# Expert layers: one ScalarE copy brings all three weight blocks of a slot, and VectorE takes over the copy of the turned rows

## The reference

```python
def _L0_ffn_ref(x, gate, experts_w1, experts_w2, experts_w3):      # layers 2 and 4: 8 experts, best 2 of a token
    routing_weights, selected = jax.lax.top_k(jnp.einsum('bsh,he->bse', x, gate), 2)
    ...
    g = jnp.einsum('bsh,ehi->ebsi', x, experts_w1)                 # 128 -> 512
    u = jnp.einsum('bsh,ehi->ebsi', x, experts_w3)                 # 128 -> 512
    eo = jnp.einsum('ebsi,eih->ebsh', silu(g) * u, experts_w2)     # 512 -> 128
    out = jnp.einsum('ebsh,bse->bsh', eo, tok_w)
```

## Time and profile before

| | us |
|---|---|
| three runs | 2781.56, 2788.8, 2790.41 (median 2788.8) |
| the profiled execution | 2790.66, its span 2788.9, mean granted clock 0.884 |
| slots of the four expert layers (first to last transposition or matmul of a slot) | 133 to 362, 545 to 775, 1710 to 1823, 2656 to 2770 |

### The profile page before, as it was taken

One profiled execution on the slowest core, in us unless ns is written; L12 is line 12 of the kernel. 1 busy time (PEld: TensorE's weight loads), 2 busy tenths in 40 slices (PEclk: granted clock), 3 DMA queues, 4 the chain that ended last, 5 costly groups with the idle time before them and its releaser, 6 DMA issues. The chain is left out here.

```text
span 2788.9 us, 78885 instructions
## 1 busy us (share of the span) xinstructions
PE 2227.6 (80%) x30447; PEld 1572.1 (56%) x30447; DVE 1813.1 (65%) x5841; ACT 1398.5 (50%) x3584; POOL 897.8 (32%) x904
## 2 busy tenths in 40 slices
PE   6499947699935888888888877948899888888686
PEld 3288835388812333333333335836777777777486
DVE  6633357633355776767867634359999999999622
ACT  5455543455521554454544445536556555555453
POOL 2156643166541101000000003534444444444254
PEclk7699979699965998988988887969999999999898
DMA  4111120111143211110110001121111111111112
GB/s 125 36 41 42 43 70 1 39 42 42 42 139 93 63 31 35 33 43 18 43 33 22 15 1 52 42 82 53 52 51 53 48 49 50 45 49 49 40 39 89
DMA packets 76684, 134.93 MB, mean 48 GB/s; under 512 B 17892, under 2 KB 32926, under 8 KB 73886
## 3 DMA queue, kind: packets, MB, share of 16 engines
q1 hardware_dynamic: 62742, 102.07, 11.6%
q0 software_dynamic: 13568, 27.81, 3.4%
q10 hardware_dynamic: 8, 0.00, 0.0%
HBM read 65.19 MB, written 32.79 MB: 35 GB/s over the span
## 5 line engine op out<-in xcount | busy, mean ns | idle before, releaser
L1499 ACT ACTIVATE ca_pt<-ca_ps 128x512 f32<-128x512 f32 (+3 forms) x768 | 341.9, 491 | 402.2 <-PE ca_ps L1601 198.8
L733 PE MATMUL ffn_ps<-ffn_xst,ffn_up_w 128*128 128x128 f32 x3392 | 420.6, 278 | 0.2 <-issue 0.2
L733 PEld LDWEIGHTS ffn_ps<-ffn_xst,ffn_up_w 128*128 128x128 f32 x3392 | 402.7, 195 | 1.2 <-issue 1.2
L856 DVE TENSOR_TENSOR ffn_hid<-ffn_sg,ffn_ps 128x512 f32<-128x512 f32 x212 | 145.8, 688 | 324.8 <-PE ffn_ps L733 234.3
L580 POOL DMA_INDIRECT ffn_y<-ffn_ys,ffn_result_at x212 | 208.8, 985 | 221.6 <-DVE ffn_ys L862 190.4
L1928 POOL TENSOR_TENSOR im_pt_e<-im_pt,im_own 128x512 f32<-128x512 f32 x128 | 162.6, 1271 | 361.9 <-DVE im_pt L2181 351.6
L575 POOL DMA_INDIRECT ffn_xs<-ffn_x,ffn_token_at x212 | 205.2, 968 | 229.7 <-DVE ffn_token_at L839 166.3
L1575 PE MATMUL ca_ps<-ca_stacks 72*128 72x512 bf16 (+3 forms) x768 | 233.3, 371 | 53.8 <-DVE ca_m_near L1721 28.2
L1597 PE MATMUL ca_ps<-ca_stacks 75*128 75x512 bf16 (+3 forms) x768 | 259.5, 361 | 16.8 <-ACT ca_pt L1499 11.2
L1720 DVE TENSOR_REDUCE ca_m_far<-ca_ps 128x1 f32<-128x128 f32 (+5 forms) x384 | 236.8, 617 | 49.7 <-PE ca_ps L1575 48.0
L1721 DVE CUSTOM_DVE_ANT_0 ca_spill<-ca_ps,ca_bias_q 128x256 f32<-128x256 f32 (+1 forms) x512 | 201.0, 397 | 32.5 <-PE ca_ps L1575 32.5
(11 more groups left out here) (332 smaller groups left out, 4897.2 us busy)
## 6 DMA issues: line engine op xcount, KB each, us to landing
im_mates<-im_t SPq DMA_DIRECT2D x256, 128.0 KB
ca_stacks<-scratch_piece SPq DMA_DIRECT2D x96, 192.0 KB
ffn_got<-ffn_y SPq DMA_DIRECT2D x48, 256.0 KB, 5.4
ffn_x<-ffn_xn SPq DMA_DIRECT2D x32, 256.0 KB, 2.0
scratch_piece<-ca_piece SPq DMA_DIRECT2D x24, 256.0 KB, 2.9
w_w<-in_L_ffn_experts_w_dram SPq DMA_DIRECT2D x2, 2048.0 KB, 12.3
ffn_xs<-ffn_x,ffn_token_at POOLq DMA_INDIRECT x212
ffn_y<-ffn_ys,ffn_result_at POOLq DMA_INDIRECT x212
```

The lines of the kernel that those rows point to most:

```text
L733: last = nc.tensor.matmul(ps[:, bank, j * P:j * P + P], up_w[:, n % WS, first + j * P:first + j * P + P], xst[:, n % 2, :], start=True, st ...
L1499: nc.scalar.activation(pt[:, i % 8, lo - c0:hi - c0], ps[:, tile_bank(i), lo - c0:hi - c0], ACT.Exp, scale=SCALE).then_inc(p_ready, 1)
```

## The change

`up_weights` becomes `copy_weights`: one ScalarE copy of 1536 columns (all three blocks) into `slot_w`, a ring of four, after a wait for y_ready of slot n-4. The three blocks of an expert must lie side by side for this, so w1, w3, w2 (and w_v, w_proj) are loaded into one tensor; the last block comes in four DMAs in place of one. PE reads only fixed addresses: `expert_of` and the register operations go. The copy to `xst` moves from ScalarE to VectorE, between `hidden(n)` and the copy to `ys`. `sg` and `hid` now use the space of `xt`, which the routing no longer needs.

```diff
-    XS, YS, WS = 6, 4, 3
+    XS, YS, WS = 6, 4, 4
...
-        sg, hid = s.sb("sg", [P, 2, CHUNK]), s.sb("hid", [P, 2, CHUNK])
-        up_w = s.sb("up_w", [P, WS, 2 * CHUNK])
+        sg, hid = xt[:, 0:2, :], xt[:, 2:4, :]
+        slot_w = s.sb("slot_w", [P, WS, 3 * CHUNK])
...
-                def turned_rows(n):
-                    act.wait_ge(S["x_turned"], n + 1)
-                    nc.scalar.activation(xst[:, n % 2, :], ps[:, 4, 0:P], ACT.Copy).then_inc(S["xst_ready"], 1)
...
                     if n >= WS:
-                        act.wait_ge(S["u_ready"], n - WS + 1)
-                    nc.scalar.activation(up_w[:, n % WS, :], up_of(e), ACT.Copy).then_inc(S["up_copied"], 1)
+                        act.wait_ge(S["y_ready"], n - WS + 1)
+                    nc.scalar.activation(slot_w[:, n % WS, :], weights_of(e), ACT.Copy).then_inc(S["weights_copied"], 1)
...
                 for n in range(SLOTS):
                     silu(n)
                     if n + 2 < SLOTS:
-                        turned_rows(n + 2)
-                        up_weights(n + 2)
+                        copy_weights(n + 2)
...
-                def expert_of(n):
-                    return nc.values_load(table_e[0:1, n:n + 1], engines=(mybir.EngineType.PE,), min_val=0, max_val=E - 1,
...
-                def rows(n, e):
+                def rows(n):
                     pe.wait_ge(S["hid_ready"], n + 1)
                     if n:
                         pe.wait_ge(S["y_copied"], n)
                     for j in range(IB):
-                        last = nc.tensor.matmul(ps[:, 5, 0:P], hid[:, n % 2, j * P:j * P + P], down(e, j), start=(j == 0), stop=(j == IB - 1))
+                        last = nc.tensor.matmul(ps[:, 5, 0:P], hid[:, n % 2, j * P:j * P + P], slot_w[:, n % WS, 2 * CHUNK + j * P:2 * CHUNK + j * P + P], start=(j == 0), stop=(j == IB - 1))
...
-                    after = expert_of(n + 1) if n + 1 < SLOTS else None
...
+                def turned_rows(n):
+                    dve.wait_ge(S["x_turned"], n + 1)
+                    nc.vector.tensor_copy(xst[:, n % 2, :], ps[:, 4, 0:P]).then_inc(S["xst_ready"], 1)
+
+                turned_rows(0)
+                turned_rows(1)
+                for n in range(SLOTS):
                     hidden(n)
-                    rows(n - 1)
+                    if n + 2 < SLOTS:
+                        turned_rows(n + 2)
+                    if n:
+                        rows(n - 1)
                 rows(SLOTS - 1)
...
-            for dst, src in ((router[:], a["L1_ffn_w_router"]), (wv[:], a["L1_ffn_w_v"].rearrange("e d h -> d e h")),
-                             (wp[:], a["L1_ffn_w_proj"].rearrange("e (b i) d -> i e b d", i=P))):
+            for dst, src in ((router[:], a["L1_ffn_w_router"]), (wvp[:, :, 0:1024], a["L1_ffn_w_v"].rearrange("e d h -> d e h")),
+                             *((wvp[:, :, 1024 + b * P:1152 + b * P], a["L1_ffn_w_proj"].rearrange("e (b i) d -> b i e d", i=P)[b]) for b in range(4))):
```

More of the change, by code:

```diff
@@ L428, in ssm_layer, with expert_layer @@
         s.clear()
-def expert_layer(nc, g, name, experts, top, weights, gate_w, up_of, down, result=None):
+def expert_layer(nc, g, name, experts, top, weights, gate_w, weights_of, result=None):
     BF, HF = mybir.dt.bfloat16, mybir.dt.float16
@@ L725, in turn_rows @@
                     nc.tensor.transpose(ps[:, 4, 0:P], xs[:, n % XS, :], g.ident[:]).then_inc(S["x_turned"], 1)
-                def expert_of(n):
-                    return nc.values_load(table_e[0:1, n:n + 1], engines=(mybir.EngineType.PE,), min_val=0, max_val=E - 1,
-                                          skip_runtime_bounds_check_because="table_e counts the experts that end before a slot and is cut at E - 1 by VectorE")
                 def up(n, first, bank):
                     for j in range(IB):
-                        last = nc.tensor.matmul(ps[:, bank, j * P:j * P + P], up_w[:, n % WS, first + j * P:first + j * P + P], xst[:, n % 2, :], start=True, stop=True)
+                        last = nc.tensor.matmul(ps[:, bank, j * P:j * P + P], slot_w[:, n % WS, first + j * P:first + j * P + P], xst[:, n % 2, :], start=True, stop=True)
                     return last
-                def rows(n, e):
+                def rows(n):
                     pe.wait_ge(S["hid_ready"], n + 1)
@@ L760, in _ @@
                     if n:
-                        rows(n - 1, before)
-                    before, e = e, after
-                rows(SLOTS - 1, before)
+                        rows(n - 1)
+                rows(SLOTS - 1)
             @block.vector
```

36 lines of the change are left out of this document (16 added, 20 removed).

## The result

The changed kernel takes 2821.91 us in the median (2806.12 to 2834.35, 12 runs), before on the same chip 2785.09 us (2779.38 to 2793.97, 12 runs). The ratio is 1.0124, with a 95% interval of 1.0105 to 1.0143. That is 37 us more, where I had forecast 35 us less. It lies within the range of 2712 to 2825, but on its other side.

A forecast was written before the change was run, and what follows sets the result against it. POOL and its DMA were taken to set the slot loops' pace, PE only waiting. Terms -36 - 0.5 + 1 + 0.5 = -35 on 2790.66 gave 2756, less 1.9: 2754 us (chance 0.40); 8-in-10 range 2712 to 2825.

The forecast's parts named there:

- All else in the span is untouched: Outside the four slot loops (698 of 2789 us) nothing changes but a few DMAs.
- I take that as the new pattern: Slot loops: three slots to a POOL ring, 8.91 us against PE's 8.37; stalls 34 us in place of 70, -36 us.
- That results ending ahead of the gather are released: Slot loops: PE results ending before the gather begins (306.84 against 306.90) get their signal at once, as read in layer 6.
- the ring stays as it is: Rival: signals just ahead of the gather are held too; PE restarts sooner, waits longer; 0 to -3, some 2787 us; chance 0.22.
- The restart: PE's restart at L741 after y_copied, 0.25 us, gets shorter by 0.05 to 0.20 us; 0.12 taken.
- No late signals: Rival: PE's register work has a part in holding signals, so all 70 us of stalls go; 2717 us; chance 0.11.
- The first slot is held too: Rival: first results of a ring end as the scatter ends and are held; +60 to +120 us, up to 2909; chance 0.20.
- ScalarE: Its weight copy grows to 1536 columns, 1.50 us; 2.10 us a slot, under PE's 2.79; cost 0.
- VectorE's copy, +1 us: Turned rows copied on VectorE, 0.29 us a slot, make `xst` 0.7 us later; +1 us, at most +10.
- The port: VectorE's new copies could shut GpSimd out of the shared port, 0.29 us each; the copies to `ys` speak against it.
- DMAs, 0 to +1: Last weight block in four DMAs in place of one: +0.9 us on a queue ahead of its users; 0 to +1.
- the path over VectorE: Rival: `xst` late where u_ready is held, or the port; 0.1 to 0.29 us a slot; 2810 to 2850 us; chance 0.07.

The follow-up runs named there:

- noreg_act: The changed kernel (no PE register, copy of 1536 columns) with the turned rows left on ScalarE; 1.0195 of before, signals held.
- after_again: The changed kernel, unchanged, run again beside before on a chip that holds PE's signals; 1.0166 of before.
- copy_first_pad116_again: The changed kernel with VectorE's copy of the results ahead of `hidden` and 116 more PE instructions ahead of the memory layer, second run; 1.0045 of before, signals held.
- after_register: The changed kernel, but PE reads the third weight block by its register as before; ScalarE still copies 1536 columns; 0.9993 of before, signals in time.
- reg_dve: The kernel before with only the copy of the turned rows moved to VectorE; 0.9977 of before, signals held.
- reg_dve_again: The kernel before with only the turned rows moved to VectorE, second run; 0.9995 of before, signals in time.
- before_layout: The kernel before with only the change's weight tensors and their four DMAs; 0.9996 of before, signals in time.
- three padded kernels: The changed kernel with 116 more PE instructions ahead of the memory layer, 1.0020; with VectorE's copy of the results also ahead of `hidden`, 1.0032 and 1.0045.

## Why the prediction was wrong

- *"All else in the span is untouched"*: this step failed first, and it was the largest that shows in both kinds of sets. No instruction of the memory layer changed, but 885 PE instructions ahead of it went, and with them the place of the fetches. I costed what an instruction takes on its engine, and not what it takes in the stream. By the table the price is 783 to 792 us in place of 762 to 773, 19 us between the means (786.4 over seven traces, 767.6 over eight), of the 37 that were measured; the expert layers' 9 to 27 make the rest. For the memory layer that is shown, by pads in both directions.
- *"I take that as the new pattern", three slots to a ring, the third held, 8.91 us*: the ring of three came, but in the profile of after only 15 times, beside 60 pairs; in noreg_act and after_again 48 and 51 times. The term mis-sized is its last gap: 4.65 to 5.0 us measured where the sum has 3.79. The sum had 0.96 us for the late signal, where the ring at 201.89 has 1.31, and 0.29 for the copy, and nothing for what stands ahead of the copy on VectorE, where it has 0.75. I had named the place ("only where u_ready is held as long as that does PE wait") and looked for the harm at `xst` alone. PE does wait there now, at its transposition; but noreg_act, with `xst` on ScalarE, is as slow, and what lengthens POOL's ring is `hidden`, ahead of `ys`. A ring is 9.8 to 10.1 us, 3.26 to 3.37 a slot, worse than the pairs. Cost: 9 us in the profile of after (an estimate from its gaps: 15 rings of 10.1 us in place of 3 x 3.18 make 8.4), 27 in after_again against copy_first_pad116_again.
- *That results ending ahead of the gather are released*: not so. In after 72 results end up to 0.16 us ahead of a gather. In 50 of these slots the copy comes 2.0 us after them, and the pair stays; in 21 it comes 0.5 to 1.3 us after them, as at 233.07. The rival "the ring stays as it is" had most of this right. Where the hold is that short, POOL loses at most 0.5 us in that slot, and a third slot can join the ring.
- *The restart, 0.05 to 0.20 us shorter*: right, 0.13 (0.25 to 0.12 us).
- *"No late signals"*, with the registers as their cause: wrong as to the cause, as two banks with all registers and noreg_act without any show them alike. They come and go with the set of runs, and they go away with the gathers.
- *"The first slot is held too"*: did not come; first results end 1.00 us after their scatter's start and are on time.
- *ScalarE*, 1.50 us a slot at no cost: right, 1.48 us, and after_register at 0.9993 carries the whole copy, with signals in time.
- *VectorE's copy, +1 us*: by itself right (reg_dve 0.9977, reg_dve_again 0.9995). In a held ring it adds its 0.28 us to the other 0.69.
- *The port*: the rule was weighed at the new copies, where it did nothing. It bit in the memory layer, between two instructions that the change doesn't name.
- *DMAs, 0 to +1*: right, before_layout 0.9996.

The signs that the prediction named for its success nearly all came: 55 waits and 40.0 us behind "issue" for about 65 and 35, the restart at 0.12 us, the copy at 1.48 us. They all lie at the places that I had looked at, and the time rose elsewhere. The sign against it, that the pairs stay, came too: there are 60 of them.

The rival "the path over VectorE", with 0.07, gave 2810 to 2850 and has the measured time in it. Its mechanism is half of what was found in the expert layers; that its number fits is luck, since it knows nothing of the 19 us in the memory layer.

What stays open: 0.2 to 0.45% in the three padded kernels with the memory layer mended. The causal layer varied from 852 to 881 us over the traces, in kernels with registers (852 to 873) and without (859 to 881), and it too follows expert layers whose PE code got shorter. The means are 861 us over nine traces with registers and 868 over eleven without; I didn't pad it, so whether this is the same effect is not shown. No kernel that does the same work on the same rows beat before by more than 0.3%: the best is reg_dve, 0.9977 and 0.9995.

## What to carry to other kernels

Taking instructions out of one stage moves every later instruction fetch; if a later stage depends on which transfer a fetch delays, it gets faster or slower by more than the edit itself. When a stage that the diff doesn't touch has changed, compare single instructions of it, and pad the stream in both kernels before believing in the edit. And when a wait is released late, look at all that is released with it: what stands ahead in the queue of the engine that was waiting, the ring pays for. With the instruction that the ring needs put first, the expert layers here took 970 us in place of 997.

## What the runs showed of the hardware that I had not expected

- A fetch of PE's instructions, 16384 bytes, takes 0.9 to 1.8 us of one DMA engine, and a small transfer over 16 engines ends as late as that engine: the last packets of `im_mates` came over a microsecond after the rest (2038.4 to 2039.5, the others by 2037.8). Five such fetches fall on four slots of the memory layer, so it is the same slot of four for some 30 slots in a row.
- While POOL issues indirect gathers, PE's signals may be held, u_ready 3.1 us in after's ring at 234.85 us, in some sets of runs and in others not at all (102 of 212 y_ready over 0.3 us, or none; chip 12 did both): 70 us of 2785, twice what the whole change cost, from nothing in the kernel.
- A VectorE product of 128x256 from two SBUF tensors took 1.34 us beside a POOL product, and 0.42 alone. It ended 0.28 us after the POOL product in every one of the 48 long cases of before and after.
